# Macaron block on one core: key sums and value products issued in one run of eight, and the work before the first scores reordered

## The reference

```
x = x + 0.5 * ffn(layernorm(x))
x = x + attention(layernorm(x))
x = x + 0.5 * ffn(layernorm(x))
```

## Time and profile before

| what | value |
|---|---|
| median of three runs | 645.0 us |
| profiled execution | 645.08 us, span 643.3 us |
| mean granted TensorE clock | 0.968 |
| PE busy | 575.6 us (89%), 3586 matmuls |
| DVE, ACT, POOL busy | 400.7, 318.4, 239.6 us |

### The profile page before, as it was taken

The page is one execution under the profiler, slowest core; times in us unless marked ns, Lnnn a source line. Parts: engine busy times, 40 slices in busy tenths (PEclk is TensorE's granted clock), DMA queues, the critical chain, the costliest instruction groups (busy, mean ns, idle before and its releaser), DMA issues.

```text
span 643.3 us, 10070 instructions
## 1 busy us (share of the span) xinstructions
PE 575.6 (89%) x3586; PEld 219.8 (34%) x3586; DVE 400.7 (62%) x782; ACT 318.4 (49%) x629; POOL 239.6 (37%) x200
## 2 busy tenths in 40 slices
PE   0483899869969999999999999999999999999876
PEld 0432545424423233233233233233333223333432
DVE  5999515616877667667667667667657842331572
ACT  1731722312226656656656656657645548572421
POOL 1511053563656547546546546546600100000100
PEclk9995889998979999999999999999999999999997
DMA  9921013550322125322223115415310003100011
GB/s 321 337 76 65 1 50 115 180 158 25 100 74 75 51 76 172 116 66 95 73 59 122 51 51 164 149 50 162 118 51 2 2 0 132 50 18 34 34 66 65
DMA packets 43553, 57.95 MB, mean 90 GB/s; under 512 B 3478, under 2 KB 34326, under 8 KB 42480
## 3 DMA queue, kind: packets, MB, share of 16 engines
q1 hardware_dynamic: 42924, 57.21, 26.7%
q10 hardware_dynamic: 580, 0.11, 0.1%
HBM read 32.01 MB, written 25.17 MB: 89 GB/s over the span
## 4 chain that ended last, share of the span: by engine, by line
PE 77%; DVE 13%; ACT 5%; issue 3%; DMA 2%; POOL 0%; SPq 0%; ACTq 0%; DVEq 0%
PE bank L901 13%; PE bank L944 12%; PE bank L1043 11%; PE bank L1033 11%; PE bank L927 10%; PE bank L855 6%; PE bank L981 5%; PE bank L865 5%; DVE stats L654 3%; ACT big L541 2%; DMA rows<-in_L_attn_x_dram 2%; DVE big L669 2%; PE bank L845 2%; DVE rmax L796 1%; ACT xh L540 1%
## 5 line engine op out<-in xcount | busy, mean ns | idle before, releaser
L796 DVE TENSOR_REDUCE rmax<-bank 128x1 f32<-128x512 f32 (+3 forms) x384 | 202.7, 553 | 128.0 <-PE bank L927 123.8
L606 ACT ACTIVATE big<-bank 128x512 f32<-128x512 f32 (+3 forms) x384 | 182.2, 490 | 151.4 <-PE bank L901 146.9
L927 PE MATMUL bank<-kst,qst 104*128 104x512 f16 (+3 forms) x384 | 126.2, 331 | 13.2 <-issue 10.2
L901 PE MATMUL bank<-qst,kst 106*128 106x512 f16 (+3 forms) x384 | 126.6, 331 | 1.6 <-ACT big L606 1.6
L499 POOL TENSOR_TENSOR rot<-t,sin_s 64x512 f32<-64x512 f32 x64 | 81.7, 1276 | 117.5 <-ACT t L599 114.9
L901 PEld LDWEIGHTS bank<-qst,kst 106*128 106x128 f16 x384 | 36.7, 96 | 137.5 <-ACT big L606 74.2
L1043 PE MATMUL bank<-big,rows 128*32 128x512 f32 (+3 forms) x768 | 81.8, 498 | 0.0
L1033 PE MATMUL bank<-big,ones 128*32 128x512 f32 (+3 forms) x768 | 81.8, 498 | 0.0
L508 POOL TENSOR_TENSOR rhl<-t,rhl 128x512 f16<-128x512 f32 x32 | 37.0, 1156 | 62.9 <-ACT rhl L620 62.9
L944 PE MATMUL bank<-xh,wh 128*128 128x512 f16 x128 | 50.0, 391 | 8.9 <-DVE xl L690 6.5
L927 PEld LDWEIGHTS bank<-kst,qst 104*128 104x128 f16 x384 | 37.8, 98 | 44.1 <-issue 14.9
(11 more groups left out here) (106 smaller groups left out, 674.6 us busy)
## 6 DMA issues: line engine op xcount, KB each, us to landing
spread<-rhl SPq DMA_DIRECT2D x32, 256.0 KB, 2.2
qst<-spread SPq DMA_DIRECT2D x16, 384.0 KB, 3.7
kst<-spread SPq DMA_DIRECT2D x16, 384.0 KB, 3.8
rows<-in_L_attn_x_dram SPq DMA_DIRECT2D x4, 1024.0 KB, 12.5
x<-rows SPq DMA_DIRECT2D x4, 1024.0 KB, 4.8
spread<-rhl SPq DMA_DIRECT2D x32, 128.0 KB, 2.1
xh<-ch SPq DMA_DIRECT2D x4, 512.0 KB, 4.2
xl<-cl SPq DMA_DIRECT2D x4, 512.0 KB, 5.4
```

The lines of the kernel that those rows point to most:

```text
L606: nc.scalar.activation(probs[:, st % P_PLACES, h, 0:n], pb[u % 2][:, 0:n], ACT.Exp, scale=EXP_SCALE).then_inc(s_eb, 1)
L796: nc.vector.tensor_reduce(rmax[:, at:at + 1], a_bank(u)[:, 0:n], AX.X, ALU.max, negate=True).then_inc(s_max, 1)
L901: nc.tensor.matmul(pb[u % 2][:, 0:n], kst[0:ROWS_B, g % SETS, h, j * P:(j + 1) * P], qst[0:ROWS_B, g % SETS, h, q0:q0 + n], start=True, st ...
L927: nc.tensor.matmul(a_bank(u)[:, 0:n], qst[0:ROWS_A, g % SETS, h, i * P:(i + 1) * P], kst[0:ROWS_A, g % SETS, h, half * HALF:half * HALF + ...
```

## The change

The constants move the A scores one step and the B scores two steps ahead, and put the value products nine steps behind instead of seven. Since 9 and 5 differ by four, the sums of one row and the value products of the row before then stand in the same step, right behind one another. The turn moves from the start of the sixth step after a head's last A unit to the end of the second; the DVE's parts of it come one unit earlier, the Ln of the sums four steps earlier than its Exp. In the prologue the first half of batch row 0 is loaded in four pieces with a semaphore each, ACT computes the columns before it converts weights, DVE's order changes, the statistics of batch row 1 move behind those of batch row 0, `weight_low` of the output weight moves into steps 16 to 19, and the feed-forward stage of batch row 1 runs four steps later. SP's writes of columns and mask rows move to steps 58, 64 and 70.

```diff
-A_START, B_START = 11, 20
-SUM_LAG, PV_LAG = 5, 7
+A_START, B_START = 10, 18
+SUM_LAG, PV_LAG = 5, 9
-MAX_PLACE = 5
+MAX_PLACE = 2
...
-        Y1_STEP = [3 + n for n in range(8)]
-        F1_STEP = [13 + 3 * r for r in range(8)]
-        S2_STEP = [26, 38]
-        N2_STEP = [30, 42]
-        X_STEP = [32 + n for n in range(4)] + [44 + n for n in range(4)]
+        SECOND = 5
+        Y1_STEP = [7 + n for n in range(8)]
+        F1_STEP = [17 + 3 * r for r in range(8)]
+        S2_STEP = [30, 42]
+        N2_STEP = [34, 46]
+        X_STEP = [36 + n for n in range(4)] + [48 + n for n in range(4)]
...
-            load_x(0, 0)
+            for r in range(4):
+                sp.dma_start(rows[0][:, r, :], x[0, r * P:(r + 1) * P, :]).then_inc(s_xtile[r], 16)
...
-                    if k == X_STEP[4 * bl + 3] + 4:
+                    if k == STEPS + 16 + 6 * bl:
                         columns_out(bl)
...
-                if k == X_STEP[7] + 4:
+                if k == STEPS + 10:
...
                     mask_rows(1, SETS)
...
-            weight_high(0)
-            weight_high(1)
             act.wait_ge(s_const, 16 * 4)
             for n in range(8):
                 columns1(0, n)
+            weight_high(0)
+            weight_high(1)
...
             statistics(0, 0, 1, *TWICE, blocks[0][0])
             weight_scale()
+            normalize(0, 0, 1, blocks[0][0], y1[0][0], s_y1[0])
             dve.wait_ge(s_x[1][0], 16)
             statistics(0, 1, 2, *TWICE, blocks[0][1])
-            ternary()
-            normalize(0, 0, 1, blocks[0][0], y1[0][0], s_y1[0])
+            ternary_above()
             normalize(0, 1, 2, blocks[0][1], y1[0][1], s_y1[0])
+            ternary_below()
+            dve.wait_ge(s_tern, 1)
             for n in range(8):
                 f_low(n, f1[0], xh, xl, s_f1[0], s_fl1[0])
-                weight_low(n // 4, n % 4)
...
+                if 16 <= k < 20:
+                    weight_low(3, k - 16)
...
-                if e := max_head(k, 1):
+                if e := max_head(k, 0):
                     n = GH * e[0] + e[1]
...
-                if e := max_head(k, MAX_PLACE + 1):
-                    n = GH * e[0] + e[1]
-                    pe.wait_ge(s_max, A_UNITS * (n + 1) + (MAX_PLACE - 2 if n + 1 < GH * ALL else 0))
-                    pe.wait_ge(s_mp, n + 1)
-                    nc.tensor.transpose(...)
                 if t := a_unit(k):
...
                     last.then_inc(s_pv, 1)
+                if e := max_head(k, MAX_PLACE):
+                    n = GH * e[0] + e[1]
+                    pe.wait_ge(s_mp, n + 1)
+                    nc.tensor.transpose(...)
```

More of the change, by code:

```diff
@@ L174, in macaron @@
         s_x = [each(f"s_x{bl}_") for bl in range(BLOCKS)]
+        s_xtile = [sem(f"s_xtile{r}") for r in range(4)]
         s_link = sem("s_link")
@@ L471, in _ @@
             pool.wait_ge(s_brow, 4)
[L472 to L475, removed]
+            rstd_of(0, 1, 2)
+            rstd_of(0, 0, 3)
+            rstd_of(0, 1, 4)
+            rstd_of(1, 0, 5)
+            rstd_of(1, 1, 6)
             roots = 6
@@ L509, in _ @@
                                        ).then_inc(s_rl, 1)
-                if c := ctx_half(k, 5):
+                if c := ctx_half(k, 4):
                     g, half = c
@@ L578, in _ @@
             for k in range(LAST_STEP):
-                if k == 2:
+                if k == SECOND + 1:
                     for n in range(4, 8):
@@ L607, in _ @@
                                          scale=EXP_SCALE).then_inc(s_eb, 1)
-                if e := max_head(k, 7):
+                if e := max_head(k, 3):
                     n = GH * e[0] + e[1]
@@ L626, in _ @@
                     nc.scalar.activation(cf[:, :], psum[:, :], ACT.Ln).then_inc(s_ln, 1)
+                if c := ctx_half(k, 0):
+                    n = 2 * c[0] + c[1]
                     act.wait_ge(s_ln, n + 1)
                     nc.scalar.activation(cf[:, :], cf[:, :], ACT.Exp, scale=-1.0).then_inc(s_rec, 1)
-                if c := ctx_half(k, 4):
+                if c := ctx_half(k, 3):
                     g, half = c
@@ L653, in statistics @@
                 for r in range(4):
+                    if n == 1:
+                        dve.wait_ge(s_xtile[r], 16)
                     last = nc.vector.bn_stats(stats[:, 4 * bl + r, :], src[:, r, :])
@@ L702, in weight_scale, with ternary_above @@
                 nc.vector.tensor_reduce(sums[:, 0:1], wf_s, AX.XY, ALU.add, apply_absolute_value=True).then_inc(s_abs, 1)
-            def ternary():
+            def ternary_above():
                 dve.wait_ge(s_tot, 1)
@@ L734, in _ @@
             normalize(0, 1, 2, blocks[0][1], y1[0][1], s_y1[0])
+            ternary_below()
+            dve.wait_ge(s_tern, 1)
             for n in range(8):
                 f_low(n, f1[0], xh, xl, s_f1[0], s_fl1[0])
-                weight_low(n // 4, n % 4)
[L738 to L742, removed]
+            ffn_update(0, f1_bank[0], blocks[0], s_ffn1[0], s_up1[0])
@@ L743, in _ @@
+            ffn_update(1, f1_bank[0], blocks[0], s_ffn1[0], s_up1[0])
+            for n in range(2):
+                weight_low(0, n)
+            ffn_update(2, f1_bank[0], blocks[0], s_ffn1[0], s_up1[0])
+            for n in range(2, 4):
+                weight_low(0, n)
+            ffn_update(3, f1_bank[0], blocks[0], s_ffn1[0], s_up1[0])
             dve.wait_ge(s_up1[0], 4)
-            statistics(0, 0, 4, *ONCE, blocks[0][0])
-            dve.wait_ge(s_x[1][1], 16)
-            statistics(1, 1, 5, *TWICE, blocks[1][1])
+            statistics(0, 0, 3, *ONCE, blocks[0][0])
@@ L747, in _ @@
+            for n in range(4):
+                weight_low(1, n)
             dve.wait_ge(s_ytr1[0], 4)
-            normalize(0, 0, 4, blocks[0][0], y1[0][0], s_y2[0])
+            normalize(0, 0, 3, blocks[0][0], y1[0][0], s_y2[0])
             for r in range(4, 8):
                 ffn_update(r, f1_bank[0], blocks[0], s_ffn1[0], s_up1[0])
-                weight_low(3, r - 4)
             dve.wait_ge(s_up1[0], 8)
-            statistics(0, 1, 6, *ONCE, blocks[0][1])
+            statistics(0, 1, 4, *ONCE, blocks[0][1])
@@ L754, in _ @@
             for n in range(4):
                 x_low(0, n)
+            for n in range(4):
+                weight_low(2, n)
             dve.wait_ge(s_ytr1[0], 8)
-            normalize(0, 1, 6, blocks[0][1], y1[0][1], s_y2[0])
-            normalize(1, 0, 6, blocks[1][0], y1[1][0], s_y1[1])
+            normalize(0, 1, 4, blocks[0][1], y1[0][1], s_y2[0])
+            dve.wait_ge(s_x[0][1], 16)
+            statistics(1, 0, 5, *TWICE, blocks[1][0])
             for k in range(LAST_STEP):
-                if k == 1:
-                    normalize(1, 1, 6, blocks[1][1], y1[1][1], s_y1[1])
-                if k == 3:
+                if k == 2:
+                    normalize(1, 0, 5, blocks[1][0], y1[1][0], s_y1[1])
+                    dve.wait_ge(s_x[1][1], 16)
+                    statistics(1, 1, 6, *TWICE, blocks[1][1])
+                if k == SECOND + 2:
@@ L889, in _ @@
             for k in range(LAST_STEP):
-                if k == 1:
+                if k == SECOND:
                     pe.wait_ge(s_y2[0], 8)
@@ L1047, in _ @@
                     last.then_inc(s_pv, 1)
+                if e := max_head(k, MAX_PLACE):
+                    n = GH * e[0] + e[1]
+                    pe.wait_ge(s_mp, n + 1)
+                    nc.tensor.transpose(max_bank(n)[0:2 * TILES, 0:P // 2].bitcast(F16),
+                                        mparts[:, n % 2, :, :].rearrange("p a t -> p (a t)"),
+                                        ident16[:, :]).then_inc(s_mtr, 1)
             for r in range(TILES):
```

15 lines of the change are left out of this document (6 added, 9 removed).

## The result

The changed kernel takes 634.49 us in the median of four runs (634.09 to 636.96), the kernel before 644.91 (644.71 to 647.46) beside it: a ratio of 0.9837 [0.9802, 0.9873], 10.4 us less. That lies in the range of 612 to 638, but 23 us less had been forecast. The profiled execution took 634.23 us, span 632.4; PE was busy for 554.8 us of it where it had been for 575.6. So PE lost 20.8 us of busy time, the run only 10.9 us of span.

The account below looks back on a forecast made before the run. PE bounds the steady periods; before them it waits for DVE and transfers. From 645.1: joins -18.0, turn -5.3, start -10, turn's wait +3, stack +3.6, Exp +3, together -23.7, gave 621.4, stated as 622; range 612 to 638.

Parts of the forecast that it names:

- Joined runs: Sums and value products side by side on PE: 0.19 us saved per pair, 95 pairs, 18.0 us (ends 0 and 22.8).
- The turn: Transpose of the maxima placed behind a run on PE: 0.19 us saved for 28 heads, 5.3 us (ends 0 and 5.9).
- Rival 1: In joined runs, second quartet's weights load only after the first; a join saves 0.08 us, total 632; chance 0.12.
- The start: Reordered prologue, set by DVE: PE's stage begins near 66.8 and waits shrink, 10 us saved (ends 5 and 13).
- PE's wait of 2.39 at 123.88 stays, as its stage moved as a whole: Prologue: this PE wait keeps its length but covers part of the later 5.80 stack wait, of which some 4 go.
- rival 2: Prologue gives nothing: DVE's savings are lost at the X transposes and first stack; 632 us; chance 0.13.
- The turn's wait: PE held at the earlier turn when L809 loses to POOL's rope: 3 us lost over six groups (ends 0 and 8.7).
- Stack and Exp: PE waits 0.6 us at the fifth A unit of groups 2 to 7, 3.6 us; B products wait for Exp, 3 us.
- Rival 3: ACT bounds the four-step cycle, delaying the third B product of each burst; 656 us at 0.4 a burst; chance 0.08.

Follow-up runs that it names:

- the start alone: The changed kernel with the old layout of scores, runs and turn, so only the reordered work before the first scores is left: 643.14 us, ratio 0.9971.
- the mends together: Changed kernel with fourth rope held behind normalizations, columns written after the fourth stack, turn at sixth step, rounding and its transfers one step earlier: 615.53 us.
- the join in the old layout: The kernel before with joined runs alone (PV_LAG 9, context steps and Ln moved to suit); start, turn and scores unchanged: 645.43 us, ratio 1.0006.

## Why the prediction came out as it did

**Joined runs: right, undersized.** 18.0 was taken, 22.3 came (0.235 a pair, by distances): the prediction paid 0.024 at each of three steps within a run, and only the first costs that (0.026), the others, the one between sums and value products too, 0.002. The turn gave 6.2 (28 times 0.22) for 5.3. So PE's side gave 28.6 for 23.3. Rival 1 is excluded by the loads at 264.44. Of the two pages weighed there, the drain of the Trainium skill, "TensorEngine Tiling (Array Packing)", "Key Properties", agrees with the trace: quartet after quartet in one mode loses 0.002, a change of mode 0.096 into a run and 0.118 out of it. The rule of the Trainium skill, "TensorE: Matmul & The Clock Gate", "The mechanism", that weight loads overlap matmuls in flight only where the row group differs, does not agree: these tiles span all rows, and the loads stand 0.42 ahead.

**The start: this step failed**, with "PE's wait of 2.39 at 123.88 stays, as its stage moved as a whole". Ten us were forecast; the start alone gave 1.8, and in the changed kernel the steady periods begin 0.6 earlier. The prologue did gain (68.00 for 69.50, less than the 66.8 worked out). But a stage that moves as a whole on PE meets other engines at other points: DVE's second normalizations now began with POOL's rope, and took 5.81 where they had taken 2.67. The wait of 5.96 ate the gain, and the half clock behind it another 2.75, which no term of the sum had; the fourth block's rounding then came behind ACT's copies, its stack was issued at 135.92 between mask rows and columns, and landed too late. In the heads of group 0 the turn's waits took 3.5 us more, where the prediction priced only six later groups. Holding back one rope gave 5.8 us; the mends together brought the unit to 134.90. This is the outcome of rival 2, at the place it named, by a mechanism it did not.

**The turn's wait: this step failed too, right in kind, wrong by 0.07 us, and so in size.** The prediction had L809 ready 1.48 after the A unit and the rope at 1.53, "0.05 us ahead". The step in it that failed is when the maximum of parts can start. The last A unit of a group's second head, and DVE's timeline and POOL's around that race:

```profile
250.36 0.38 PE L939 MATMUL bank<-kst,qst 104*128 104x512 f16 x1
```
```profile
251.61 0.16 DVE L825 TENSOR_TENSOR rmax<-rmax 128x4 f32<-128x4 f32 x1
251.80 0.17 DVE L827 TENSOR_SCALAR mparts<-rmax 128x8 f16<-128x8 f32 x1
252.01 1.17 DVE L828 SCALAR_TENSOR_TENSOR mparts<-rmax,mparts 128x8 f16<-128x8 f32 x1
```
```profile
251.88 2.61 POOL L502 TENSOR_TENSOR rot<-t,sin_s 64x512 f32<-64x512 f32 x2 [2.33 <-ACT t L602]
```

L828 starts 1.65 after the A unit here, and is held until POOL's first half is through. In the first, third and fourth heads it starts 1.54 after the A unit (by the trace's starts), 0.06 later than the 1.48 worked out, when the rope has begun at 1.52. So the race was lost in every head with a rope, and the cost is what the prediction gave for losing: 0.54 + 0.85 + 0 + 0.22 measured a group, for 0.48 + 0.80 + 0 + 0.17. It took 3 us for what the view shows as 9.9 (group 0 included) and the runs as 7.0 and 7.6. An even race should have stood at both ends, not at a mean near the winning one.

**Stack and Exp: about right.** The stack was priced at 0.6 in groups 2 to 7, 3.6 us; it measured about 0.8 in the view (4.7 of six), 1.0 to 1.1 in distances. B's waits are 2.2 us in the view and 4.7 in distances (2.6 before), for 3.0. Rival 3 did not come about in the changed kernel, but the join in the old layout shows that it was real: there waits took 19 of the 22 us, and the run was no faster. Why the new order of steps escapes it was not tried part by part; scores one step closer, sums and lags moved at once.

In sums: -23.3 + 9.6 - 10 = -23.7 was forecast; -28.6 + 18.2 - 0.6 = -11.0 came.

## What to carry to other kernels

Price a change of the array's mode by distances of starts, not by busy times, and join runs of one mode; but what PE saves appears only so far as engines behind it keep up, so look for the short waits that follow (here the join paid nothing in one layout, 14 us in another). When a stage is moved earlier on its own engine, go through every shared event that it starts from, and ask which other engine starts from the same one. Count a long wait of PE with the clock behind it, not by its length alone. A race that is 0.05 us from even is to be taken as lost, or ordered by a semaphore: here small edits against such collisions, one step of one chain among them, gave 19 us, more than the change itself.

## What the runs showed of the hardware

- A small DVE operation with two inputs in SBUF (128x8) takes 0.167 us, or 1.28 when a POOL operation on SBUF began 0.02 us ahead of it: it is held for the whole of that operation. The Trainium skill's "GPSIMD Engine Reference", "Specifications", names the shared interfaces for such operations, without a price; the trace agrees.
- DVE's normalization of 128x512 f32 takes 0.48 by itself (1.92 for four) and 1.45 beside a rope on POOL (5.81 for four), about one POOL operation of 1.3 to each.
- Within PE's wait of 5.96 us the granted clock fell from full (2.4 GHz) to half (1.2 GHz), and stayed there for 6.8 us, in all six profiled runs that have this wait; behind waits of 2.07 to 2.4 it stayed at full in five runs of six. The products behind the long wait took 10.81 us for 8.06.
- Two kinds of products in the same mode with different weights follow each other at 0.002 us beyond columns, as the halves within a run do; a change of mode costs 0.096 going in, 0.026 at the first step and 0.118 coming out. The weights of the second kind are loaded 0.42 us ahead.
